# A recurrent cell's state products from fp16 parts, theta computed earlier, two sums merged, preparation reordered

## The chip, the cores and the metric

The kernel runs on one core of a Trainium2 chip. Its time is the device time of one execution, in microseconds (us), as a median over runs. The core has five engines that run their own instruction streams and wait for each other through semaphores: TensorE (PE, its weight loads shown as PEld), VectorE (DVE), ScalarE (ACT), GpSimd (POOL) and SyncE (SP), which issues most DMAs.

## The reference

2048 sequences of 256 steps go through a recurrent cell. In each step, with the carried state `st` (32 values), error, gate (8 values), a memory of the last 20 inputs and two LSTM cells:

```python
encoded = jnp.tanh(xt @ We + st @ Ue + be)
new_state = jnp.tanh(jnp.einsum('bd,cds->bcs', xt, Wx) + jnp.einsum('bs,cst->bct', st, Ws) + bk)
inp = jnp.concatenate([encoded, err[:, None]], axis=1)
mem = jnp.concatenate([inp[:, None, :], mem[:, :-1, :]], axis=1)
a = jax.nn.relu(mem.reshape(b, -1) @ enc_w1 + enc_b1)
agent_in = jax.nn.relu(a @ enc_w2 + enc_b2)
h1, c1 = _lstm_cell(agent_in, h1, c1, ...)
h2, c2 = _lstm_cell(h1, h2, c2, ...)
gate = jax.nn.softmax(h2 @ gate_w + gate_b, axis=1)
theta = _clamp01(jnp.mean(jnp.abs(mem[:, :10, -1]), axis=1) * 2.5)[:, None]
gate = gate * theta + gs * (1.0 - theta)
st = jnp.einsum('bc,bcs->bs', gate, new_state)
pred = _clamp01(st[:, -1])
err = pred - yt
```

The output is `pred` of every step, as fp32.

## The kernel before

The 2048 sequences are cut into two groups of 1024, a group into eight tiles of 128 sequences (`HF` 2 by `Q` 4). A work item is one step of one group, so there are 512 items. The engines handle them in phases, one new item in each: `run_phases` keeps the last three items, called new, cur and old, and each engine's `phase` function does its part of all three in a fixed, hand-written order. An engine runs its list strictly in that order. The first two items and the last two phases lie outside a loop of 51 turns with five steps of both groups (ten phases) each.

What an item goes through, with the lines at which it is recorded:

- TensorE transposes the state (`state_transpose`, L293, two matmuls) and the prediction (L305), ScalarE copies the state to SBUF (`state_take`, L498), TensorE adds W_e's and U_e's products (`encoded_x` L320, `encoded_s` L327), and ScalarE makes the encoded input and its fp16 high part (L504, L511); GpSimd makes the low part (`entry_low`, L944), which SyncE stores in the history.
- The first encoder layer is `history` (L378, fp16 parts) and `encoder1_now` (L389), the second is L400. Two LSTM cells follow: products `cell_gates` (L417), ScalarE's tanhs (L550, L555, L560), VectorE's `cell_terms` (L705), `cell_value` (L711), `first_hidden` (L720, two instructions) and `second_hidden` (L729).
- The candidates of the new state get their bias (L340), x's part from fp16 pieces that GpSimd splits (`x_high` L933, `x_low` L938; products L350, 24 of them: weight high by x high, weight low by x high, weight high by x low) and the state's part in fp32 (L359: eight products, recorded as 16). ScalarE takes their tanh (`candidates`, L536, one instruction for each quarter).
- The logits (L427, L434) go to VectorE (`peaks` L752, `below_peak` L757), ScalarE (L574), VectorE (`totals`, `reciprocals`) and GpSimd (`weighted_exponentials`, L891, which multiplies by theta), then `fresh_gate` (L774) and `new_gate` (L781) on VectorE and `gate_in_sbuf` (L899) on GpSimd. Theta comes from `error_sum` (L681) and `thetas` (L687); GpSimd makes 1-theta and the kept part of the old gate from it (`kept_share` L877, `kept_gate` L884).
- The mix of candidates by the gate is split: VectorE multiplies half of it (L792), GpSimd two quarters of it (`mix_quarter` 1, then 0, L911). VectorE sums over the candidates in four `mix_sum` (L810), clamps the prediction (`prediction`, L818), and GpSimd forms the new error (`new_error`, L968) and keeps the prediction (`keep_prediction`, L977).

VectorE's order in a phase: totals, reciprocals, fresh_gate, new_gate (old); agent_input (cur); mix, sum (old); cell_terms 0, cell_value 0 (cur); sum (old); first_hidden (cur); two sums (old); error_sum (cur); prediction (old); cell_terms 1, cell_value 1 (cur); errors (new); second_hidden, thetas, peaks, below_peak (cur). GpSimd's order: gate_in_sbuf, two mix quarters (old); x_high, x_low (new); next_hidden (L921, old); kept_share, kept_gate (cur); new_error, keep_prediction (old); entry_low (new); weighted_exponentials (cur). `x_high` waits for `first_hidden` by choice, to keep away from VectorE's work.

Before the first item VectorE splits biases (L637 to L641) and the history's weight table (L647, L648) into fp16 parts, scales weights and marks the preparation as done (L676). SyncE then issues the first three sets of history weights (L223), without which TensorE can't start.

Of the kernel before, what the change touches and what calls it, by code (L numbers as in the profile page):

```python
# [41 lines left out]
def recurrent_kernel(nc, x_l, y_l, y, error0, gate0, w, ident_c, columns_c, out):  # L42
    ctx = ExitStack()
    with ctx:
# [18 lines left out]
        w_s = sb("w_s", [P, NS])  # L63
        w_x_parts = sb("w_x_parts", [P, 2, NS], FP16)
# [12 lines left out]
        ones = sb("ones", [P, TILES])  # L77

# [47 lines left out]
        s_out, s_ys, s_hist0 = sem("s_out"), sem("s_ys"), sem("s_history_zero")  # L126
        s_x = [sem(f"s_x_slot{u}") for u in range(PER_TILE)]
# [22 lines left out]
        q_xh, q_xl = sem("q_xh"), sem("q_xl")  # L150
        q_bias = [sem(f"q_bias{c}") for c in range(2)]
        q_hkept = sem("q_hkept")
        q_sum = [[sem(f"q_sum{hf}_{pair}") for pair in range(2)] for hf in range(HF)]
# [45 lines left out]
        def _(sp):  # L199
# [11 lines left out]
            for t in range(PER_TILE):  # L211
                sp.dma_start(x_sb[:, t, :, :].rearrange("p g b -> p (g b)"), x_l[P * t:P * t + P, :])\
                    .then_inc(s_x[t], 16)
                sp.dma_start(y_rows[0:Q, t, :, :].rearrange("p g b -> p (g b)"), y_l[Q * t:Q * t + Q, :])\
                    .then_inc(s_y[t], 16)


            sp.wait_ge(s_parts, 1)
            sp.dma_start(gate_bias[1:2, :], gate_bias_low[0:1, :]).then_inc(s_fix, 16)
            sp.dma_start(cand_bias[1:P:D_IN, :], cand_bias_low[0:P:D_IN, :]).then_inc(s_fix, 16)  # L220
# [6 lines left out]
            sp.wait_ge(s_ready, 1)  # L227
            history_weights(w_slot(-1), PER_TILE)
            history_weights(0, PER_TILE + 1)
            history_weights(1, PER_TILE + 2)  # L230

# [53 lines left out]
        def _(pe):  # L285
            pe.wait_ge(s_ready, 1)
            pe.wait_ge(s_fix, 16 * 2)

            def state_transpose(item, hf):
                g, n, u = item  # L290
                for pair in range(2):
                    pe.wait_ge(q_sum[hf][pair], n)
# [41 lines left out]
            def candidates_bias(item):  # L334
                g, n, u = item
                for q in CAND_ORDER:
                    pe.wait_ge(q_cand[q], n)
# [16 lines left out]
            def candidates_s(item):  # L354
                g, n, u = item
                for hf in range(HF):
                    for q in range(Q):
                        rows = slice(D_IN * q, D_IN * q + D_IN)
                        last = nc.tensor.matmul(cand_ps[q][:, NS * hf:NS * hf + NS],  # L359
                                                state_t[rows, g, P * hf:P * hf + P], w_s[rows, :],  # L360
                                                start=False, stop=True, skip_group_check=True)
# [82 lines left out]
            def phase(items, extra):  # L444
# [21 lines left out]
                if cur:  # L466
                    cell_gates(cur, 0)
                    candidates_bias(cur)
# [11 lines left out]
        def _(act):  # L480
# [11 lines left out]
            act.dma_start(ys[:, :, :], y.rearrange("(n p) t -> p n t", p=P)).then_inc(s_ys, 16)  # L492
            act.wait_ge(s_ready, 1)
# [115 lines left out]
        def _(dve):  # L609
            V = nc.vector  # L610
            V.memset(err_ring[:, :, :], 0.5).then_inc(s_zero, 1)

# [10 lines left out]
            for hf in range(HF):  # L623
                for pair in range(2):
                    V.memset(state[:, :, hf, 2 * pair:2 * pair + 2, :], 0.0).then_inc(q_sum[hf][pair], GROUPS)
            V.memset(scratch[:, :, :], 0.0).then_inc(s_prep, 1)
            dve.wait_ge(s_prep, 1)
            dve.wait_ge(s_biases, 16 * 2)
# [3 lines left out]
            def link(ins):  # L632
# [4 lines left out]
            link(V.tensor_copy(cand_bias[:, :], bk_stage))  # L637
            link(V.tensor_tensor(cand_bias_low[:, :], bk_stage, cand_bias[:, :], ALU.subtract))

            link(V.tensor_copy(gate_bias[0:1, :], gate_bias_stage[0:1, :]))  # L640
            V.tensor_tensor(gate_bias_low[0:1, :], gate_bias_stage[0:1, :], gate_bias[0:1, :], ALU.subtract)\  # L641
                .then_inc(s_parts, 1)

# [6 lines left out]

# [9 lines left out]
            link(V.tensor_scalar(cell_bias[:, :, 0:3], cell_bias[:, :, 0:3], 0.5, None, ALU.mult))  # L660
            link(V.tensor_copy(w_x_parts[:, 0, :], w_x[:, :]))
# [14 lines left out]
            V.tensor_copy(scratch[:, 1, :], ones[:, :]).then_inc(s_ready, 1)  # L676

# [134 lines left out]

            def prediction(item):
                g, n, u = item
                for hf in range(HF):
                    for pair in range(2):
                        dve.wait_ge(q_sum[hf][pair], n + GROUPS)
# [6 lines left out]
            def phase(items, extra):  # L824
# [19 lines left out]
                if old:  # L844
                    mix_sum(old, 1, 0)
                    mix_sum(old, 1, 1)
# [4 lines left out]
                if cur:  # L851
                    cell_terms(cur, 1)
# [6 lines left out]
                if cur:  # L859
                    second_hidden(cur)  # L860
                    thetas(cur)
# [6 lines left out]
        def _(pool):  # L868
# [71 lines left out]

            def entry_low(item):
# [44 lines left out]
            def phase(items, extra):  # L986
# [114 lines left out]
```

## Time and profile before

| | us |
|---|---|
| median of 3 runs | 5336.49 (5336.03 to 5337.18) |
| profiled execution | 5342.21 |
| its span | 5340.3 |
| granted TensorE clock, share of full speed | 0.998 |
| busy: PE, DVE, ACT, POOL | 5165.0, 4468.2, 4233.4, 3060.8 |

The profile is of one execution. Its span runs from the first to the last instruction of the program; the execution's own time is a little longer. A busy share counts the time in which an engine works on instructions; matmuls overlap, and their ends are modelled, so two rows of TensorE can overlap. A timeline row gives the start in us from the span's start, the duration, the engine and line, the operation, what it writes and reads, and how many instructions the row merges; in brackets stands how long the engine was idle ahead of it, and for whom it waited.

### The profile page before, as it was taken

The page shows a single profiled execution, that of the slowest core. Times are in us where ns is not written, and L with a number is a line of the kernel's source. Part 1 is how long each engine was busy: PE and PEld are TensorE (multiplying, and loading weights), DVE is VectorE, ACT ScalarE, POOL GpSimd, SP SyncE. Part 2 cuts the span into 40 slices and gives each one's busy share as a digit, 9 for nine tenths or more (in the row PEclk, how much of TensorE's full clock was granted, in tenths as well). Part 3 has the DMA queues.
Part 4 walks back from the last instruction along what each step waited for, and adds up shares of the span by engine and source line. Part 5 has one row for each costly group of instructions (what it writes and reads, how often), then busy time and mean ns, then how long its engine had stood idle before and what let it go on. Part 6 is the DMA issues. An engine that isn't in the chain of part 4 may idle for free.

```text
span 5340.3 us, 193942 instructions
## 1 busy us (share of the span) xinstructions
PE 5165.0 (97%) x68608; PEld 3158.5 (59%) x68608; DVE 4468.2 (84%) x11824; ACT 4233.4 (79%) x10241; POOL 3060.8 (57%) x6149
## 2 busy tenths in 40 slices
PE   7999999999999999999999999999999999999998
PEld 4555555555555555555555555555555555555554
DVE  7888888888888888888888888888888888888887
ACT  6887877878888878788787788788877878777886
POOL 4555555555555555555555555555555555555555
PEclk9999999999999999999999999999999999999999
DMA  2111111111111111111111111111111111111111
GB/s 68 31 30 33 30 33 30 33 30 33 30 33 30 31 31 30 33 30 33 30 33 30 33 30 33 30 32 30 30 33 30 33 30 33 30 33 30 33 30 41
DMA packets 299271, 172.29 MB, mean 32 GB/s; under 512 B 156598, under 2 KB 263866, under 8 KB 298698
## 3 DMA queue, kind: packets, MB, share of 16 engines
q1 hardware_dynamic: 293560, 159.45, 11.9%
q8 instruction: 564, 9.24, 0.7%
q10 hardware_dynamic: 5138, 3.53, 0.2%
q14 instruction: 9, 0.07, 0.0%
HBM read 74.55 MB, written 2.10 MB: 14 GB/s over the span
## 4 chain that ended last, share of the span: by engine, by line
PE 94%; ACT 4%; issue 2%; DVE 0%; DMA 0%; POOL 0%; ACTq 0%; POOLq 0%; DVEq 0%
PE a_ps L378 27%; PE chain L417 21%; PE a_ps L389 9%; PE cand_ps L359 8%; PE cand_ps L350 6%; PE chain L327 6%; PE chain L320 4%; ACT state_t L498 4%; PE chain L293 4%; PE a_ps L400 3%; PE cand_ps L340 3%; PE chain L434 1%; PE chain L427 0%; DMA gate_bias_stage<-in_gate_b 0%; DVE enc_table L648 0%
## 5 line engine op out<-in xcount | busy, mean ns | idle before, releaser
L378 PE MATMUL a_ps<-hist,w_hist 125*64 125x512 f16 x12288 | 1816.5, 383 | 25.2 <-DMA w_hist<-enc_table 24.0
L810 DVE TENSOR_REDUCE state<-mixed 128x64 f32<-128x512 f32 x2048 | 1353.4, 682 | 34.2 <-POOL mixed L911 0.8
L911 POOL TENSOR_TENSOR mixed<-cand,gate 128x512 f32<-128x512 f32 x1024 | 1285.3, 1277 | 48.6 <-POOL gate L899 12.5
L417 PEld LDWEIGHTS chain<-cell_in,cell_w 128*64 128x64 f32 x16384 | 903.2, 136 | 488.7 <-ACT cell_in L525 248.5
L417 PE MATMUL chain<-cell_in,cell_w 128*64 128x128 f32 x16384 | 1120.5, 277 | 41.5 <-issue 1.4
L536 ACT ACTIVATE cand<-cand_ps 128x512 f32<-128x512 f32 x2048 | 1107.0, 594 | 13.3 <-issue 0.4
L378 PEld LDWEIGHTS a_ps<-hist,w_hist 125*64 125x64 f16 x12288 | 695.8, 109 | 568.8 <-issue 298.1
L933 POOL CAST x_parts<-x_sb 128x256 f16<-128x256 f32 x512 | 203.8, 398 | 953.2 <-DVE cell_in L720 938.4
L550 ACT ACTIVATE gates<-chain 128x384 f32<-128x384 f32 x1024 | 503.5, 492 | 251.2 <-PE chain L417 251.2
L705 DVE SCALAR_TENSOR_TENSOR added<-gates 128x256 f32<-128x256 f32 x1024 | 620.8, 606 | 57.2 <-ACT gates L550 3.7
L877 POOL TENSOR_TENSOR one_theta<-ones,theta 128x8 f32<-128x8 f32 x512 | 105.3, 206 | 950.0 <-DVE theta L687 950.0
L543 ACT ACTIVATE chain<-cell_bias 128x512 f32<-128x512 f32 x1024 | 611.0, 597 | 16.1
L792 DVE TENSOR_TENSOR mixed<-cand,chain 128x1024 f32<-128x1024 f32 x512 | 616.4, 1204 | 0.2 <-issue 0.2
L560 ACT ACTIVATE tanh_c<-gates 128x128 f32<-128x128 f32 x1024 | 318.8, 311 | 305.1 <-DVE gates L711 305.0
L389 PE MATMUL a_ps<-entry,w_now 100*64 100x256 f32 x4096 | 555.0, 388 | 0.0
L359 PE MATMUL cand_ps<-w_s,state_t 32*128 32x256 f32 x8192 | 529.3, 375 | 0.0
L350 PE MATMUL cand_ps<-w_x_parts,x_parts 32*128 32x256 f16 x12288 | 421.5, 268 | 0.0
L327 PE MATMUL chain<-state_t,w_ue 128*64 128x256 f32 x2048 | 334.1, 405 | 87.4 <-ACT state_t L498 87.1
L517 ACT ACTIVATE a_sb<-a_ps,columns 128x512 f32<-128x512 f32 x512 | 352.3, 688 | 69.6 <-PE a_ps L389 0.8
L359 PEld LDWEIGHTS cand_ps<-w_s,state_t 32*128 32x128 f32 x8192 | 356.5, 186 | 24.7
L938 POOL TENSOR_TENSOR x_parts<-x_sb,x_parts 128x256 f16<-128x256 f32 x512 | 344.6, 673 | 41.1
L350 PEld LDWEIGHTS cand_ps<-w_x_parts,x_parts 32*128 32x128 f16 x12288 | 315.7, 93 | 71.7
(80 smaller groups left out, 7348.5 us busy)
## 6 DMA issues: line engine op xcount, KB each, us to landing
x_sb<-in_x_l SPq DMA_DIRECT2D x260, 256.0 KB, 2.7
hist<-entry_parts SPq DMA_DIRECT2D x2048, 25.0 KB
w_hist<-enc_table SPq DMA_DIRECT2D x258, 128.0 KB, 2.4
y_rows<-in_y_l SPq DMA_DIRECT2D x260, 8.0 KB
ys<-in_y ACTq DMA_DIRECT2D x1, 2048.0 KB, 16.7
preds_out<-preds SPq DMA_DIRECT2D x1, 2048.0 KB, 7.5
cand<-in_encoder ACTq DMA_DIRECT2D x1, 640.0 KB, 3.8
cell_w<-in_cell ACTq DMA_DIRECT2D x2, 256.0 KB, 5.3
```

Of the source, the lines that this page charges most:

```text
L327: last = nc.tensor.matmul(chain[g][rows, Z_AT:Z_AT + COLS], w_ue[:, rows], state_t[:, g, :], start=False, stop=True, skip_group_check=True)
L350: nc.tensor.matmul(cand_ps[q][:, NS * hf:NS * hf + NS], x_parts[rows, g, xp, P * hf:P * hf + P], w_x_parts[rows, wp, :], start=False, stop ...
L359: last = nc.tensor.matmul(cand_ps[q][:, NS * hf:NS * hf + NS], state_t[rows, g, P * hf:P * hf + P], w_s[rows, :], start=False, stop=True, ...
L378: nc.tensor.matmul(a_ps[g][ENC * half:ENC * half + ENC, :], w_hist[0:HROWS, w_slot(u), kk, wp, :], hist[0:HROWS, xp, k, at:at + 512], star ...
L389: last = nc.tensor.matmul(a_ps[g][rows, COLS * p:COLS * p + COLS], w_now[0:ER, p, rows], entry[0:ER, g, :], start=False, stop=True, skip_g ...
L417: last = nc.tensor.matmul(chain[g][rows, P * r:P * r + P], cell_w[c][:, hf, r, :], cell_in[c][:, g, hf, :], start=False, stop=True, skip_g ...
L536: ins = nc.scalar.activation(cand[:, g, q // 2, :, q % 2, :, :].rearrange("p h s c -> p h (s c)"), cand_ps[q][:, :].rearrange("p (h k) -> ...
L543: nc.scalar.activation(chain[g][:, :].rearrange("p (r b) -> p r b", r=4), cell_bias[:, c, :].rearrange("p (r o) -> p r o", o=1).to_broadca ...
L705: V.scalar_tensor_tensor(added[c][:, g, :, :], gates[c][:, g, 1:3, :], 1.0, gates[c][:, g, 3:5, :], ALU.add, ALU.mult).then_inc(q_added[c], 1)
L792: V.tensor_tensor(mixed[:, 1, :, :, :, :].rearrange("p h l s c -> p (h l) s c"), cand[:, g, 1, :, :, :, :].rearrange("p h l s c -> p (h l) ...
L810: V.tensor_reduce(state[:, g, hf, 2 * pair:2 * pair + 2, :], mixed[:, pair, hf, :, :, :], AX, ALU.add)\
L911: G.tensor_tensor(mixed[:, 0, :, q, :, :], cand[:, g, 0, :, q, :, :], over_s, ALU.mult)\
```

## The change

Six edits. The state's part of the candidates uses fp16 pieces: `w_s` is split once, and for each item GpSimd makes a high and a low part of the transposed state (`state_high`, `state_low`); TensorE does 24 fp16 products in place of the fp32 ones and waits for the low part. `thetas` stands directly behind `prediction` on VectorE. GpSimd's `new_error` and `keep_prediction` stand ahead of `kept_share` and `kept_gate`, and the two new functions come after these, ahead of `entry_low`. The last two sums of an item are one instruction, `last_sums`. In the preparation the history weights' DMAs are issued as soon as their table is split, x and y of slots 1 to 4 and the bias rows behind them; the biases are split after the mark, and only the first candidates wait for them. ScalarE does a small Tanh before it waits for the mark.

```diff
@@ tiles and semaphores
+        w_s_parts = sb("w_s_parts", [P, 2, NS], FP16)
+        state_parts = sb("state_parts", [P, GROUPS, 2, COLS], FP16)
+        warm = sb("warm", [P, 2, TILES])
-        q_sum = [[sem(f"q_sum{hf}_{pair}") for pair in range(2)] for hf in range(HF)]
+        q_sum = [[sem(f"q_sum0_{pair}") for pair in range(2)], [sem("q_sum1")]]
@@ sync
-            sp.wait_ge(s_parts, 1)
-            sp.dma_start(gate_bias[1:2, :], gate_bias_low[0:1, :]).then_inc(s_fix, 16)
-            sp.dma_start(cand_bias[1:P:D_IN, :], cand_bias_low[0:P:D_IN, :]).then_inc(s_fix, 16)
-            sp.wait_ge(s_ready, 1)
+            load_slot(0)
+            sp.wait_ge(s_tables, 1)
             history_weights(w_slot(-1), PER_TILE)
             history_weights(0, PER_TILE + 1)
             history_weights(1, PER_TILE + 2)
+            for t in range(1, PER_TILE):
+                load_slot(t)
+            sp.wait_ge(s_parts, 1)
+            sp.dma_start(gate_bias[1:2, :], gate_bias_low[0:1, :]).then_inc(s_fix, 16)
+            sp.dma_start(cand_bias[1:P:D_IN, :], cand_bias_low[0:P:D_IN, :]).then_inc(s_fix, 16)
+            sp.wait_ge(s_ready, 1)
@@ tensor
             pe.wait_ge(s_ready, 1)
-            pe.wait_ge(s_fix, 16 * 2)
-            def candidates_bias(item):
+            def candidates_bias(item, extra):
                 g, n, u = item
+                if extra is None:
+                    pe.wait_ge(s_fix, 16 * 2)
             def candidates_s(item):
                 g, n, u = item
+                pe.wait_ge(q_sl, n)
                 for hf in range(HF):
-                    for q in range(Q):
-                        rows = slice(D_IN * q, D_IN * q + D_IN)
-                        last = nc.tensor.matmul(cand_ps[q][:, NS * hf:NS * hf + NS],
-                                                state_t[rows, g, P * hf:P * hf + P], w_s[rows, :],
-                                                start=False, stop=True, skip_group_check=True)
+                    for t, (wp, xp) in enumerate(PIECES):
+                        for q in range(Q):
+                            rows = slice(D_IN * q, D_IN * q + D_IN)
+                            last = nc.tensor.matmul(cand_ps[q][:, NS * hf:NS * hf + NS],
+                                                    state_parts[rows, g, xp, P * hf:P * hf + P],
+                                                    w_s_parts[rows, wp, :], start=False,
+                                                    stop=(t == len(PIECES) - 1), skip_group_check=True)
@@ scalar, before the wait for s_ready
+            act.wait_ge(s_warm, 1)
+            nc.scalar.activation(warm[:, 1, :], warm[:, 0, :], ACT.Tanh)
@@ vector, preparation (the four bias instructions now stand behind s_ready)
+            V.tensor_copy(scratch[:, 1, :], ones[:, :]).then_inc(s_tables, 1)
...
+            link(V.tensor_copy(w_s_parts[:, 0, :], w_s[:, :]))
+            link(V.tensor_tensor(w_s_parts[:, 1, :], w_s[:, :], w_s_parts[:, 0, :], ALU.subtract))
@@ vector
+            def last_sums(item):
+                g, n, u = item
+                dve.wait_ge(q_mul[1], n + GROUPS)
+                for q in range(2):
+                    dve.wait_ge(q_mulpool[q], n + GROUPS)
+                V.tensor_reduce(state[:, g, 1, :, :].rearrange("p (a l) s -> p a (l s)", a=2),
+                                mixed[:, :, 1, :, :, :].rearrange("p a l s c -> p a (l s) c"), AX, ALU.add)\
+                    .then_inc(q_sum[1][0], 1)
@@ vector, phase
                 if old:
-                    mix_sum(old, 1, 0)
-                    mix_sum(old, 1, 1)
+                    last_sums(old)
                 if cur:
                     error_sum(cur)
                 if old:
                     prediction(old)
                 if cur:
+                    thetas(cur)
                     cell_terms(cur, 1)
...
                     second_hidden(cur)
-                    thetas(cur)
                     peaks(cur)
@@ gpsimd
+            def state_high(item):
+                g, n, u = item
+                pool.wait_ge(s_ready, 1)
+                pool.wait_ge(q_st, n)
+                G.tensor_copy(state_parts[:, g, 0, :], state_t[:, g, :]).then_inc(q_sh, 1)
+
+            def state_low(item, other):
+                g, n, u = item
+                pool.wait_ge(q_sh, n)
+                if other:
+                    pool.wait_ge(q_h[1], n - 1)
+                G.tensor_tensor(state_parts[:, g, 1, :], state_t[:, g, :], state_parts[:, g, 0, :],
+                                ALU.subtract).then_inc(q_sl, 1)
@@ gpsimd, phase
                 if old:
                     next_hidden(old, cur)
+                    new_error(old, extra)
+                    keep_prediction(old, extra)
                 if cur:
                     kept_share(cur)
                     kept_gate(cur)
-                if old:
-                    new_error(old, extra)
-                    keep_prediction(old, extra)
+                if new:
+                    state_high(new)
+                    state_low(new, cur)
                 if new:
                     entry_low(new)
```

## Rows read from the trace of the kernel before

**Rows 1.** The page, busy time by engine.
```profile
PE 5165.0 (97%) x68608; PEld 3158.5 (59%) x68608; DVE 4468.2 (84%) x11824; ACT 4233.4 (79%) x10241; POOL 3060.8 (57%) x6149
```
**Rows 2.** Timeline of TensorE, two phases of the loop; start and duration in us.
```profile
2157.78 0.44 PE L293 MATMUL chain<-ident,state 128*128 128x128 f32 x2
...
2159.85 0.32 PE L434 MATMUL chain<-gate_w,h_second 128*64 128x64 f32 x4
...
2166.22 0.60 PE L320 MATMUL chain<-x_sb,w_we 128*64 128x256 f32 x4
2166.86 1.09 PE L417 MATMUL chain<-cell_in,cell_w 128*64 128x128 f32 x16
...
2168.10 0.44 PE L293 MATMUL chain<-ident,state 128*128 128x128 f32 x2
...
2178.38 0.44 PE L293 MATMUL chain<-ident,state 128*128 128x128 f32 x2
```
**Rows 3.** The chain of waits in the first of them; start, length.
```profile
2164.31 0.65 PE cand_ps L350 x24
2164.97 0.87 PE cand_ps L359 x16
...
2166.39 0.43 PE chain L320 x4
```
**Rows 4.** Timeline of VectorE, the same phases.
```profile
2157.88 0.20 DVE L818 TENSOR_SCALAR pred_now<-state 128x8 f32<-128x8 f32 x1
2158.19 0.42 DVE L705 SCALAR_TENSOR_TENSOR added<-gates 128x256 f32<-128x256 f32 x1
...
2159.49 0.29 DVE L729 SCALAR_TENSOR_TENSOR h_second<-gates,tanh_c 128x128 f32<-128x128 f32 x1
2159.70 0.17 DVE L687 TENSOR_SCALAR theta<-err_sum 128x8 f32<-128x8 f32 x1
...
2161.81 0.23 DVE L774 TENSOR_TENSOR fresh<-weighted,recip 128x64 f32<-128x64 f32 x1 [0.33 <-POOL weighted L891]
2162.07 0.23 DVE L781 TENSOR_TENSOR chain<-fresh,kept 128x64 f32<-128x64 f32 x1
...
2164.55 0.79 DVE L705 SCALAR_TENSOR_TENSOR added<-gates 128x256 f32<-128x256 f32 x1
...
2166.18 0.57 DVE L720 SCALAR_TENSOR_TENSOR cell_in<-gates,tanh_c 64x128 f32<-64x128 f32 x2
2166.79 1.28 DVE L810 TENSOR_REDUCE state<-mixed 128x64 f32<-128x512 f32 x2
...
2174.88 0.74 DVE L705 SCALAR_TENSOR_TENSOR added<-gates 128x256 f32<-128x256 f32 x1
```
**Rows 5.** Timeline of GpSimd, the same phases.
```profile
2157.66 0.40 POOL L921 COPY cell_in<-cell_in 128x256 f32<-128x256 f32 x1
...
2160.78 0.67 POOL L944 TENSOR_TENSOR entry_parts<-entry,entry_parts 128x256 f16<-128x256 f32 x1
2161.41 0.30 POOL L891 TENSOR_TENSOR weighted<-expd,theta 128x64 f32<-128x64 f32 x1
2162.11 0.36 POOL L899 TENSOR_TENSOR gate<-fresh,kept 128x64 f32<-128x64 f32 x1 [0.41 <-DVE fresh L774]
2162.55 2.51 POOL L911 TENSOR_TENSOR mixed<-cand,gate 128x512 f32<-128x512 f32 x2
...
2172.83 2.51 POOL L911 TENSOR_TENSOR mixed<-cand,gate 128x512 f32<-128x512 f32 x2
```
**Rows 6.** Timeline of ScalarE, candidate 0 in the first phase.
```profile
2162.82 0.60 ACT L536 ACTIVATE cand<-cand_ps 128x512 f32<-128x512 f32 x1
```
**Rows 7.** Timeline of the first 35 us: mark, first products, table load.
```profile
21.23 0.16 DVE L676 COPY scratch<-ones 128x8 f32<-128x8 f32 x1
...
24.01 3.62 PE L378 MATMUL a_ps<-hist,w_hist 125*64 125x512 f16 x16 [24.01 <-DMA w_hist<-enc_table]
...
29.45 1.28 ACT L498 ACT_TABLE_LOAD   x1 [29.45 <-PE chain L293]
```

More of the change, by code:

```diff
@@ L126, in recurrent_kernel @@
         s_out, s_ys, s_hist0 = sem("s_out"), sem("s_ys"), sem("s_history_zero")
+        s_tables, s_warm = sem("s_tables"), sem("s_warm")
         s_x = [sem(f"s_x_slot{u}") for u in range(PER_TILE)]
@@ L150, in recurrent_kernel @@
         q_xh, q_xl = sem("q_xh"), sem("q_xl")
+        q_sh, q_sl = sem("q_sh"), sem("q_sl")
         q_bias = [sem(f"q_bias{c}") for c in range(2)]
         q_hkept = sem("q_hkept")
-        q_sum = [[sem(f"q_sum{hf}_{pair}") for pair in range(2)] for hf in range(HF)]
+        q_sum = [[sem(f"q_sum0_{pair}") for pair in range(2)], [sem("q_sum1")]]
         block = ctx.enter_context(nc.Block())
@@ L210, in _, with load_slot @@
                 load(err_ring[:, :, 0:1], error0.rearrange("(n p o) -> p n o", p=P, o=1))
-            for t in range(PER_TILE):
+            def load_slot(t):
                 sp.dma_start(x_sb[:, t, :, :].rearrange("p g b -> p (g b)"), x_l[P * t:P * t + P, :])\
@@ L286, in _ @@
             pe.wait_ge(s_ready, 1)
-            pe.wait_ge(s_fix, 16 * 2)
             def state_transpose(item, hf):
                 g, n, u = item
-                for pair in range(2):
-                    pe.wait_ge(q_sum[hf][pair], n)
+                for done in q_sum[hf]:
+                    pe.wait_ge(done, n)
                 last = nc.tensor.matmul(chain[g][:, P * hf:P * hf + P],
@@ L467, in phase @@
                     cell_gates(cur, 0)
-                    candidates_bias(cur)
+                    candidates_bias(cur, extra)
                     candidates_x(cur)
@@ L610, in _ @@
             V = nc.vector
+            V.memset(warm[:, 0, :], 0.0).then_inc(s_warm, 1)
             V.memset(err_ring[:, :, :], 0.5).then_inc(s_zero, 1)
@@ L622, in _ @@
                 V.memset(gates[n][:, :, 4, :], 0.0)
-            for hf in range(HF):
-                for pair in range(2):
-                    V.memset(state[:, :, hf, 2 * pair:2 * pair + 2, :], 0.0).then_inc(q_sum[hf][pair], GROUPS)
+            for pair in range(2):
+                V.memset(state[:, :, 0, 2 * pair:2 * pair + 2, :], 0.0).then_inc(q_sum[0][pair], GROUPS)
+            V.memset(state[:, :, 1, :, :], 0.0).then_inc(q_sum[1][0], GROUPS)
             V.memset(scratch[:, :, :], 0.0).then_inc(s_prep, 1)
             dve.wait_ge(s_prep, 1)
-            dve.wait_ge(s_biases, 16 * 2)
             steps = [1]
@@ L635, in link @@
                 dve.wait_ge(s_prep, steps[0])
[L637 to L642, printed above, removed]
             dve.wait_ge(s_table, 16)
@@ L676, in _ @@
             V.tensor_copy(scratch[:, 1, :], ones[:, :]).then_inc(s_ready, 1)
+            dve.wait_ge(s_biases, 16 * 2)
+            link(V.tensor_copy(cand_bias[:, :], bk_stage))
+            link(V.tensor_tensor(cand_bias_low[:, :], bk_stage, cand_bias[:, :], ALU.subtract))
+            link(V.tensor_copy(gate_bias[0:1, :], gate_bias_stage[0:1, :]))
+            V.tensor_tensor(gate_bias_low[0:1, :], gate_bias_stage[0:1, :], gate_bias[0:1, :], ALU.subtract)\
+                .then_inc(s_parts, 1)
             def error_sum(item):
@@ L815, in prediction @@
                 for hf in range(HF):
-                    for pair in range(2):
-                        dve.wait_ge(q_sum[hf][pair], n + GROUPS)
+                    for done in q_sum[hf]:
+                        dve.wait_ge(done, n + GROUPS)
                 V.tensor_scalar(pred_now[:, g, :].rearrange("p (h q) -> p h q", h=HF), state[:, g, :, :, S - 1],
```

## The prediction

> **What bounds the kernel now.** I read the page's busy shares first, then the chain of waits, then the timelines of the four engines over two phases of the steady loop, then the first 30 us. A phase is one work item of one group: 512 of them, each about 10.3 us. The page calls TensorE 97% busy [rows 1] and the chain runs through matmuls almost alone, so at first sight every nanosecond of TensorE counts. The timelines say otherwise. Take the phase that starts with the state transpose at 2157.78 and ends with the next at 2168.10 (10.32 us), and the one after it, to 2178.38 (10.28 us) [rows 2]. I give times as offsets from the phase's start.
>
> Near its end stand four W_e products (L320), begun at 8.44; they take 0.43 [rows 2, 3], so TensorE could go on at 8.87. The second cell's products (L417) begin only at 9.08 [rows 2]. They wait for `first_hidden` (L720) on VectorE, which ends at 8.97 (2166.18+0.57) [rows 4]; 0.11 later the products start, and 1.24 after them the next transpose [rows 2]. That gap of 0.21 is invisible in the chain, because modelled ends of matmuls cover it. Why does L720 end then? VectorE runs in order from `cell_terms` of cell 0 (L705): in the middle of the phase it takes 0.79, not the 0.42 of the same instruction at 2158.19 [rows 4]. It ends at 2165.34, 0.28 after GpSimd's two mixes (2162.55+2.51 = 2165.06) [rows 4, 5]. In the next phase: mixes end at 2175.34, L705 at 2175.62, again 0.28, while its duration is another (0.74). So L705, which reads two SBUF operands, stands still until GpSimd's mix is done, and then runs its whole stream. The cycle is then: mix end + 0.28 + 1.41 (L705's end to L720's) + 0.11 + 1.24 = mix end + 3.04. It gives 2168.10 and 2178.38, exactly both transposes [rows 2]. What sets the time is when GpSimd finishes the mixes.
>
> The Trainium skill (Trainium Kernel Development and Optimization, Performance Expectations) says that matmul busy time is a bad metric of distance from the roof because matmuls are pipelined. The trace agrees: 97% busy, and 0.21 of each phase is a pause. By the opposite reading the change would bring the full saving of its matmuls, which is rival 1.
>
> Going back from the mixes: they start 0.74 after `fresh_gate` (L774) does (2161.81 to 2162.55), and L774 starts 0.10 after GpSimd's `weighted_exponentials` (L891, 3.63 to 3.93) [rows 4, 5]. L891 is late because theta comes late: VectorE makes it (L687) only behind `second_hidden`, at 1.92, and behind it GpSimd has five instructions in a row up to L944, the subtraction (0.67) that ends at 3.67 [rows 4, 5].
>
> **The change, part by part.**
> *State products in fp16.* Out: the 0.87 of L359. In: 24 fp16 products of the same tiles as L350's, 0.65 [rows 3]. TensorE saves 0.22 a phase. By itself this only widens the pause. Its new wait for the low part delays nothing: the state's parts are ready by about 2.8 (below) and the products start at 7. Behind this wait everything of TensorE would queue, with 4 us of cover.
>
> *Theta behind the prediction.* Theta (0.17) falls between `prediction` (L818, which ends at 0.30) and L705 at 0.41 [rows 4]; L687 starts 0.08 before its predecessor ends, as at 2159.70, so it is done at 0.39 and L705, which waits for ScalarE's gates, isn't moved. Its cover is this gap; without it the cost would be 0.17 at most. Nothing is waiting on VectorE at its old place (it waits for logits there).
>
> *GpSimd's queue.* The six instructions from `kept_share` to `weighted` stood behind theta (done at 2.09). Now `new_error` starts at 0.30+0.08 = 0.38, then `keep_prediction`, then theta's two, at about 0.15, 0.15, 0.3 from start to start, all before 1.5 instead of from 2.16 on. Added: the fp16 copy of the state (0.40, as L921 for 256 elements) and the subtraction (0.67, as L944) [rows 5]. The copy waits for the state at about 0.86 and then the queue, and runs at 1.45 to 1.85. The subtraction waits for `second_hidden` (end 2.00 [rows 4]) and starts 0.08 after it. Behind these two waits stand `entry_low` and `weighted`.
>
> *Collisions.* What the new order adds is GpSimd work during `cell_terms`, `cell_value` and `second_hidden`, which all read two SBUF operands. `new_error` starts at 0.38, L705 at 0.41 [rows 4]. By the 0.28 rule just read, L705 ends at 0.60+0.28 = 0.88 instead of 0.83: +0.05. The trace has no short GpSimd instruction under such an L705, so the bounds are 0 (the small ones hold nothing) and 0.34 (rival 4). The reverse also occurs: `gate_in_sbuf` (L899), begun 0.04 after `new_gate` (L781), takes 0.36 where L891 of the same shape takes 0.30 [rows 4, 5]; whoever starts first holds the other. I take 0.05. Then `second_hidden` ends at 2.05 and the logits (L434 at 2.07 [rows 2]) start 0.07 after it, at 2.12.
> The Trainium skill (SBUF — State Buffer, Who interferes with whom) has this rule: a VectorE instruction with two SBUF inputs contends with a GpSimd instruction that reads SBUF, and the one issued first has the shared ports for its whole duration. It speaks against this change, which puts four more such instructions there; by it L705 would lose what remains of `new_error`, near the 0.05 taken from the rows.
>
> *Sum.* State subtraction 2.13; `entry_low` 0.63 later (pitch of L944 to L891 [rows 5]) at 2.76; `weighted` at 3.39 to 3.69; `fresh_gate` at 3.79 instead of 4.03; the mixes 4.53 to 7.04. The second mix (half of 2.51 and a little, 1.28) also needs candidate 0, which ScalarE (L536) ends at 5.64 [rows 6], 5.69 behind the later logits, and 0.08 more to GpSimd: not before 5.77, end 7.05. So this floor is just reached, and earlier weights would bring nothing more. Mix end: 7.28 becomes 7.05; phase: 10.09, a gain of 0.23. In the other phase of the pair the mixes start at 4.73 [rows 2, 5], 0.04 earlier; it meets the floor at 10.05, gain 0.23 too. TensorE's own road is now 8.87-0.22+1.24 = 9.89, below both; with L359 left in fp32 it would be 10.11, so the fp16 split is what lets the last 0.02 to 0.06 be had.
> 512 x 0.23 = 118 us.
>
> *Last two sums in one.* Two take 1.28 [rows 4]. One of 1024 elements: between 1.20 (one start less, an estimate) and 1.28; taken 1.21. They end 0.1 before TensorE asks, so 0 on the path.
>
> *Preparation.* The history weights are now issued once the tables are split, not behind the final mark (L676, done at 21.39), so TensorE, which began at 24.01 when they landed [rows 7], can begin near 21.4: -2.6. Bias splitting goes behind the mark, fp16 parts of W_s come before it; I take these as equal. The eight DMAs of x and y slots 1 to 4 go behind the weights, their first use is a phase or more later. The two bias DMAs come after the mark and have some 10 us until the first candidates. An early Tanh moves the table load (1.28 [rows 7]) under the loads: -1.3. Together -4, bounds 0 and -7.
>
> Total: -118 - 4 = -122. The profiled execution took 5342.2 (span 5340.3), so it would become 5220; it lies 5.7 above the median shown, 5336.5, and from that the forecast is 5215.
>
> **Rivals.**
> 1. *TensorE is the bound after all.* For it: 97% busy and the chain. Against: the pause of 0.21 and the exact 3.04. 512 x 0.22 = 113, with preparation 5220; the steps of GpSimd would then not matter. The time hardly differs from mine, the trace would.
> 2. *No collisions.* Short instructions hold nothing. Both phases stand at the floor of candidate 0, 5.72+1.28+3.04 = 10.04: gain 0.28 and 0.24, mean 0.26: 133+4, 5200.
> 3. *The gain is eaten by waiting in GpSimd's queue.* If L705 gets in first (a margin of 0.03), `new_error` waits until 0.83, each of the next waits for the next VectorE instruction, the copy of the state runs against `second_hidden` and ends near 2.3, and `weighted` ends near 3.92, where it was (3.93). Gain 0: 5332. A middle case: the copy gets in first, holds `second_hidden` until about 2.2, and the gain sinks to 0.08: 41+4, 5291.
> 4. *Slower: VectorE is held behind the whole string.* GpSimd's four short instructions follow each other without a gap; if the waiting L705 can't get in between, it ends at about 0.90+0.28 = 1.18, `second_hidden` at 2.34 and the logits start at 2.41, +0.34 (0.27 in the other phase), and GpSimd's road goes on from there: subtraction 2.42, `entry_low` 3.05, `weighted` 3.68 to 3.98, `fresh_gate` 4.08, mix end 7.33, phase 10.37 against 10.32 (10.31 against 10.28 in the other). 512 x 0.04 = 20, less 4: 5352. It is slower than before from a hold of about 0.3 on. For it: GpSimd's records overlap by 0.06. Against: the instruction that has waited longest should be next.
>
> **Chances.** Forecast 0.42; rival 1 0.11; rival 2 0.14; rival 3 0.13 at no gain, 0.10 in the middle; rival 4 0.10. A measurement of this kernel can tell 0.2% (10.7 us) from nothing: faster (below 5325.8) 0.42+0.11+0.14+0.10 = 0.77, within it 0.13, slower 0.10. The range: from 5190 (below rival 2, with a preparation of -7 and rounding) up to 5335, since without the case of no gain 0.23 would be left out. The likeliest case alone: 5200 to 5240.
>
> **What would show it.** In the profile after: phases of about 10.07; the mixes ending at about 7.0 and L705 still 0.28 behind them; `weighted` ending near 3.7; the first L705 0.47 rather than 0.42; GpSimd's second mix starting 0.08 behind candidate 0; TensorE still pausing before L417. Wrong: L705 of cell 1 over 0.6, or `second_hidden` past 2.1 (rival 4, middle case); `weighted` at 3.9 (rival 3); no pause before L417 at a shorter phase (rival 1).

## The result, and the profile after

The changed kernel takes 5296.3 us (5296.1 to 5296.6, 4 runs) against 5336.8 before: ratio 0.9924, interval 0.9907 to 0.9942. It is faster by 40 us where 122 were forecast. The profiled execution's span is 5294.5 instead of 5340.3, 45.8 less; that is more than 40 because the profiled execution of the kernel before took 5342.2, 5.4 more than its median here. In the span, the first state transpose comes 3.3 us earlier (25.5 instead of 28.8), and the 511 distances from transpose to transpose are 10.246 us on average instead of 10.331: 43.4 us. Of these, 1.6 come from the first distance alone (9.92 instead of 11.50). The stretch behind the last transpose is 1.0 longer. Averages over the loop in this text are taken over 472 of its phases in a run's trace.

The page's busy time by engine, as [rows 1]:

```profile
PE 5097.5 (96%) x72704; PEld 2994.3 (57%) x72704; DVE 4465.8 (84%) x11315; ACT 4215.9 (80%) x10242; POOL 3684.6 (70%) x7173
```

TensorE has 67 us less of busy time and GpSimd 624 more. Neither number is near 40. One phase tells more; it starts at 2156.75 (TensorE's timeline, as [rows 2]; lines have moved, L428 is the cells' products, L299 the state's transpose, L369 the new fp16 products):

```profile
2156.75 0.44 PE L299 MATMUL chain<-ident,state 128*128 128x128 f32 x2
...
2158.96 0.34 PE L445 MATMUL chain<-gate_w,h_second 128*64 128x64 f32 x4
...
2163.87 0.82 PE L369 MATMUL cand_ps<-w_s_parts,state_parts 32*128 32x256 f16 x24
...
2165.08 0.60 PE L326 MATMUL chain<-x_sb,w_we 128*64 128x256 f32 x4
2165.75 1.09 PE L428 MATMUL chain<-cell_in,cell_w 128*64 128x128 f32 x16
2166.99 0.44 PE L299 MATMUL chain<-ident,state 128*128 128x128 f32 x2
```

The logits (L445) start 2.21 after the phase's start, not at 2.07 as before. The fp16 products are as cheap as forecast: their 0.82 above includes overlap, and in the chain of waits they take 0.66, where the fp32 ones took 0.87 [rows 3]:

```profile
2164.04 0.66 PE cand_ps L369 x24
```

Yet L428 still waits: L326's 0.43 end at 2165.51, L428 starts at 2165.75, a pause of 0.24 (0.21 before). VectorE's timeline, as [rows 4] (L720 is `cell_terms`, L842 `prediction`, L702 theta, L744 `second_hidden`, L735 `first_hidden`):

```profile
2156.79 0.26 DVE L842 TENSOR_SCALAR pred_now<-state 128x8 f32<-128x8 f32 x1
2156.97 0.16 DVE L702 TENSOR_SCALAR theta<-err_sum 128x8 f32<-128x8 f32 x1
2157.16 0.43 DVE L720 SCALAR_TENSOR_TENSOR added<-gates 128x256 f32<-128x256 f32 x1
...
2158.47 0.44 DVE L744 SCALAR_TENSOR_TENSOR h_second<-gates,tanh_c 128x128 f32<-128x128 f32 x1
...
2163.63 0.61 DVE L720 SCALAR_TENSOR_TENSOR added<-gates 128x256 f32<-128x256 f32 x1
```

and GpSimd's, as [rows 5] (L1005 `new_error`, L968 and L975 the state's copy and subtraction, L914 `weighted_exponentials`, L934 the mixes):

```profile
2157.27 0.40 POOL L1005 TENSOR_TENSOR err_ring<-pred_now,ys 128x8 f32 x1 [0.24 <-DVE pred_now L842]
2157.61 0.20 POOL L1014 COPY preds<-pred_now 128x8 f32 x1
2157.76 0.29 POOL L900 TENSOR_TENSOR one_theta<-ones,theta 128x8 f32<-128x8 f32 x1
2158.13 0.29 POOL L907 TENSOR_TENSOR kept<-gate,one_theta 128x64 f32<-128x64 f32 x1
2158.36 0.40 POOL L968 CAST state_parts<-state_t 128x256 f16<-128x256 f32 x1
2159.05 0.67 POOL L975 TENSOR_TENSOR state_parts<-state_t,state_parts 128x256 f16<-128x256 f32 x1 [0.29 <-DVE h_second L744]
2159.68 0.67 POOL L981 TENSOR_TENSOR entry_parts<-entry,entry_parts 128x256 f16<-128x256 f32 x1
2160.31 0.29 POOL L914 TENSOR_TENSOR weighted<-expd,theta 128x64 f32<-128x64 f32 x1
2161.01 0.36 POOL L922 TENSOR_TENSOR gate<-fresh,kept 128x64 f32<-128x64 f32 x1 [0.41 <-DVE fresh L789]
2161.45 2.51 POOL L934 TENSOR_TENSOR mixed<-cand,gate 128x512 f32<-128x512 f32 x2
```

The cycle is the one read before: mixes end at 2163.96, `cell_terms` 0.28 later (2164.24, held again: 0.61), the next transpose 3.03 after the mixes' end. But `new_error` starts at 0.52 of the phase, not 0.38, so `cell_terms` (0.41) comes first and is not held (0.43), while `new_error` takes 0.40 instead of 0.22. It ends 0.07 after `cell_terms`, and it does so in the whole loop, in the four phases of five where it starts 0.21 behind the prediction as in the fifth, where it starts 0.32 behind: once it comes second, its own start no longer counts. GpSimd's string is that much later, the state's copy runs from 2158.36 to 2158.76, and `second_hidden`, begun at 2158.47, stands until then: 0.44 instead of 0.29. It ends 0.15 after the copy, in every phase of the loop. That moves the logits by 0.14 (0.11 on average over the loop), and the state's subtraction, which waits for `second_hidden`, with them. The rows show this hold; what it is worth, and what each part of the change does, the runs below tell.

### The profile page after: what moved, and what is told of

Same layout as the page of the kernel before. It is cut to its first block, busy times and chain, and to the rows that moved or that the text cites. A ratio compares the mean times of both kernels' runs of the same rounds, so it can differ in the third digit from the quotient of the medians.

```text
span 5294.5 us, 202648 instructions
## 1 busy us (share of the span) xinstructions
PE 5097.5 (96%) x72704; PEld 2994.3 (57%) x72704; DVE 4465.8 (84%) x11315; ACT 4215.9 (80%) x10242; POOL 3684.6 (70%) x7173
## 4 chain that ended last, share of the span: by engine, by line
PE 93%; ACT 4%; issue 2%; DVE 0%; POOL 0%; DMA 0%; POOLq 0%; DVEq 0%; ACTq 0%
PE a_ps L389 27%; PE chain L428 21%; PE a_ps L400 8%; PE cand_ps L358 6%; PE cand_ps L369 6%; PE chain L333 6%; PE chain L326 4%; ACT state_t L511 4%; PE chain L299 4%; PE a_ps L411 3%; PE cand_ps L348 3%; PE chain L445 3%; PE chain L438 0%; DVE enc_table L653 0%; DMA cand<-in_encoder 0%
## 5 line engine op out<-in xcount | busy, mean ns | idle before, releaser
L934 POOL TENSOR_TENSOR mixed<-cand,gate 128x512 f32<-128x512 f32 x1024 | 1283.6, 1275 | 51.4 <-POOL gate L922 12.8
L428 PEld LDWEIGHTS chain<-cell_in,cell_w 128*64 128x64 f32 x16384 | 904.0, 136 | 516.5 <-issue 268.2
L428 PE MATMUL chain<-cell_in,cell_w 128*64 128x128 f32 x16384 | 1121.3, 277 | 67.0 <-issue 13.7
L389 PEld LDWEIGHTS a_ps<-hist,w_hist 125*64 125x64 f16 x12288 | 637.5, 109 | 562.8 <-issue 212.0
L825 DVE TENSOR_REDUCE state<-mixed 128x64 f32<-128x512 f32 x1024 | 698.4, 682 | 19.6 <-POOL mixed L934 1.9
L833 DVE TENSOR_REDUCE state<-mixed 128x128 f32<-128x1024 f32 x512 | 624.7, 1220 | 15.8
L720 DVE SCALAR_TENSOR_TENSOR added<-gates 128x256 f32<-128x256 f32 x1024 | 540.5, 528 | 21.2 <-ACT gates L563 4.0
L400 PE MATMUL a_ps<-entry,w_now 100*64 100x256 f32 x4096 | 530.9, 379 | 0.0
L975 POOL TENSOR_TENSOR state_parts<-state_t,state_parts 128x256 f16<-128x256 f32 x512 | 344.1, 672 | 149.2 <-DVE h_second L744 149.1
L369 PE MATMUL cand_ps<-w_s_parts,state_parts 32*128 32x256 f16 x12288 | 421.7, 268 | 0.0
```

What stands on the lines that cost most here:

```text
L389: nc.tensor.matmul(a_ps[g][ENC * half:ENC * half + ENC, :], w_hist[0:HROWS, w_slot(u), kk, wp, :], hist[0:HROWS, xp, k, at:at + 512], star ...
L400: last = nc.tensor.matmul(a_ps[g][rows, COLS * p:COLS * p + COLS], w_now[0:ER, p, rows], entry[0:ER, g, :], start=False, stop=True, skip_g ...
L428: last = nc.tensor.matmul(chain[g][rows, P * r:P * r + P], cell_w[c][:, hf, r, :], cell_in[c][:, g, hf, :], start=False, stop=True, skip_g ...
L825: V.tensor_reduce(state[:, g, hf, 2 * pair:2 * pair + 2, :], mixed[:, pair, hf, :, :, :], AX, ALU.add)\
L833: V.tensor_reduce(state[:, g, 1, :, :].rearrange("p (a l) s -> p a (l s)", a=2), mixed[:, :, 1, :, :, :].rearrange("p a l s c -> p a (l s) ...
L934: G.tensor_tensor(mixed[:, 0, :, q, :, :], cand[:, g, 0, :, q, :, :], over_s, ALU.mult)\
```

## The experiments

Every run is given with the median of the kernel before that was measured with it. These medians differ by up to 6 us, on one chip too, so runs are compared by their ratios. No run is numbered e8.

| run | us | before | ratio (interval) |
|---|---|---|---|
| changed kernel | 5296.3 | 5336.8 | 0.9924 (0.9907 to 0.9942) |
| e1, state in fp32 | 5219.4 | 5340.9 | 0.9773 (0.9757 to 0.9790) |
| e2, a third of the products | 5324.7 | 5340.9 | 0.9968 (0.9956 to 0.9979) |
| e3, copy on ScalarE | 5229.3 | 5340.9 | 0.9792 (0.9775 to 0.9808) |
| e4, copy behind second_hidden | 5472.7 | 5340.9 | 1.0247 (1.0230 to 1.0264) |
| e5, short mix (on the kernel before) | 5210.2 | 5336.0 | 0.9762 (0.9746 to 0.9779) |
| e6, theta back | 5735.4 | 5336.0 | 1.0746 (1.0729 to 1.0764) |
| e7, fixed address | 5237.1 | 5336.0 | 0.9812 (0.9796 to 0.9829) |
| e9, e3 with one wait | 5221.4 | 5336.0 | 0.9784 (0.9767 to 0.9800) |
| e10, e9 with candidate 0 early | 5196.7 | 5342.0 | 0.9729 (0.9716 to 0.9743) |
| e11, e1 with candidate 0 early | 5252.0 | 5342.0 | 0.9834 (0.9821 to 0.9848) |
| e12, preparation and sums only | 5336.4 | 5342.0 | 0.9990 (0.9981 to 0.9999) |

**e5: is it the end of the mixes?** In the kernel before, half of GpSimd's second mix is left out; these products stay zero.

```diff
+            V.memset(mixed[:, :, :, :, :, :].rearrange("p a h l s c -> p (a h l s c)"), 0.0)
...
-                over_s = gate[:, g, q:Q:2, :]...to_broadcast([P, HF, S, C])
-                G.tensor_tensor(mixed[:, 0, :, q, :, :], cand[:, g, 0, :, q, :, :], over_s, ALU.mult)
+                some = HF if q == 1 else 1
+                over_s = gate[:, g, q:q + 2 * some - 1:2, :]...to_broadcast([P, some, S, C])
+                G.tensor_tensor(mixed[:, 0, 0:some, q, :, :], cand[:, g, 0, 0:some, q, :, :], over_s, ALU.mult)
```


> The kernel before the change, with half of GpSimd's second mix left out (quarter 0 of one half; these products stay zero). Its mixes end 0.6 us earlier in each phase, TensorE's work is untouched. Theory (the mix's end releases VectorE's cell_terms and sets the phase): cell_terms of cell 0 runs in 0.42 us and the phase falls from 10.33 us to TensorE's own road, 10.09 as the fp32 run showed: 5341 - 123 = about 5218. Rival (TensorE's matmuls bind): no change, 5341.

5210, ratio 0.9762. TensorE's work is that of the kernel before, and 126 us are gone. GpSimd's timeline, the short second mix, VectorE's `cell_terms` after it, and TensorE's products:

```profile
2149.82 0.72 POOL L913 TENSOR_TENSOR mixed<-cand,gate 128x256 f32<-128x256 f32 x1
```
```profile
2150.53 0.41 DVE L706 SCALAR_TENSOR_TENSOR added<-gates 128x256 f32<-128x256 f32 x1
```
```profile
2152.20 0.60 PE L320 MATMUL chain<-x_sb,w_we 128*64 128x256 f32 x4
2152.63 1.04 PE L417 MATMUL chain<-cell_in,cell_w 128*64 128x128 f32 x16
```

The mix ends at 2150.54 and `cell_terms` isn't held. L417 follows L320 after 0.43, without a pause. The mean phase is 10.070, now TensorE's own road with fp32 products. So the 97% of [rows 1] hid a wait.

**e2: is it TensorE?** 16 of the 24 state products are left out.

```diff
-                    for t, (wp, xp) in enumerate(PIECES):
+                    for t, (wp, xp) in enumerate(PIECES[:1]):
...
-                                                    stop=(t == len(PIECES) - 1), skip_group_check=True)
+                                                    stop=(t == 0), skip_group_check=True)
```


> The changed kernel with 16 of the 24 state products of each item left out (only high by high is computed), which takes 0.43 us a phase from TensorE. Theory: TensorE is not the bound, it pauses longer before the second cell's products; 5296 within 5. Rival (TensorE is the bound): 512 x 0.43 = 220 us less, about 5076.

5325, slower than the changed kernel, not faster. Eight of ten phases of a loop turn are as long as there (10.25 and 10.22). TensorE's waits (in total, times, longest) show the pause before the second cell's products, which lies open here, at 0.52 in every phase:

```profile
PE chain L428 <- issue: 265.3, 511, 0.7
```

The tenth, at the turn's end, takes 10.79 on average instead of 10.29, and the one behind it 10.19 instead of 10.33: 0.36 a turn, 18 us in 51 turns. That is the loss of the profiled execution (5313.9), the fastest of seven; the other six lie between 5322 and 5325, and for what they lose beyond it there is no trace. At the turn's end the transpose comes up to 3.95 behind the mixes' end and not 3.04, so there TensorE is late by itself. Why the turn's end costs more with fewer instructions in it was not found out.

**e1: the split undone.** The fp32 products are back, and `state_high` and `state_low` are gone:

```diff
-                pe.wait_ge(q_sl, n)
...
-                if new:
-                    state_high(new)
-                    state_low(new, cur)
```


> The changed kernel with one part undone: the state's products in fp32 again (0.87 us a phase on TensorE instead of 0.65), and GpSimd neither copies nor subtracts the state. Theory (the time is set by when GpSimd ends its mixes, and the fp16 copy of the state holds second_hidden for 0.15 us a phase): second_hidden ends at 2.00 again, weighted_exponentials at 3.6, GpSimd's second mix starts at its floor behind candidate 0 (5.72 us after the phase's start) and ends at 7.00; the cycle over the mixes is 10.04 us, TensorE's own road with fp32 10.11. Phase about 10.12 instead of 10.25: 5296 - 65 = about 5232. Rival (TensorE's work is the bound): 512 x 0.22 us come back, about 5408.

5219, ratio 0.9773: the split costs this kernel 1.5%, and what is left, theta's place with GpSimd's new order, brings 2.2% (e1 less the 0.1% of e12). How much of it is theta's place and how much GpSimd's order was not run apart. Nothing holds `second_hidden` (0.29), and `weighted_exponentials` ends 0.24 earlier on average over the loop. GpSimd's and TensorE's timelines:

```profile
2150.14 2.58 POOL L931 TENSOR_TENSOR mixed<-cand,gate 128x512 f32<-128x512 f32 x2
```
```profile
2155.76 0.44 PE L299 MATMUL chain<-ident,state 128*128 128x128 f32 x2
```

The next transpose is 3.04 behind the mixes' end (2152.72). The two mixes take 2.58, not 2.51: the second waits for candidate 0, so this is the floor, 10.088 in nine of ten phases. It lies 0.02 above TensorE's own road with fp32 products, 10.07 in e5; the prediction had put that road at 10.11.

**e4 and e6: GpSimd's queue.** In e4 the copy waits for `second_hidden` too; in e6 theta is back at its old place.

```diff
                 pool.wait_ge(q_st, n)
+                if other:
+                    pool.wait_ge(q_h[1], n - 1)
```


> The changed kernel, but GpSimd's fp16 copy of the state also waits for second_hidden, so it can't hold it. Theory (both the hold and GpSimd's queue up to weighted_exponentials count): second_hidden at 2.00, but copy and subtraction follow it, weighted_exponentials ends at about 4.18 instead of 3.85 us after the phase's start, mixes at 7.53, phase 10.57: 5296 + 165 = about 5460. Rival (the hold is the whole loss): 0.13 us a phase less, about 5229.


```diff
-                    thetas(cur)
                     cell_terms(cur, 1)
...
                     second_hidden(cur)
+                    thetas(cur)
```


> The changed kernel with one part undone: thetas stands behind second_hidden again, all else as changed. Theory (GpSimd's queue up to weighted_exponentials sets the mixes): one_theta starts at 2.17 us of the phase, kept at 2.45, copy and subtraction of the state 2.7 to 3.85, weighted ends at 4.73 instead of 3.85, mixes at 8.1, phase 11.1: 5296 + 450 = about 5750. Rival (theta's place is worth no more than its 0.17 us on VectorE): 5296 within 20.

5473 and 5735, both within 15 of the expectation. In e4 nothing holds `second_hidden`, and still the phase is 10.59, because `weighted_exponentials` comes 0.35 later. The hold alone is thus not what counts; the queue up to `weighted_exponentials` is. In e6 the string of six stands behind theta (GpSimd's timeline):

```profile
2160.17 0.21 POOL L900 TENSOR_TENSOR one_theta<-ones,theta 128x8 f32<-128x8 f32 x1 [1.12 <-DVE theta L702]
...
2162.43 0.30 POOL L914 TENSOR_TENSOR weighted<-expd,theta 128x64 f32<-128x64 f32 x1
```

With all parts of the change but theta's move, the kernel is thus 7.5% slower than before: the parts are far from additive.

**e7: the step that failed.** `new_error` with constant columns and one wait, so that GpSimd computes no address behind the wait. It follows neither the ring nor the step.

```diff
                 pool.wait_ge(q_pred, n + GROUPS)
-                pool.wait_ge(q_errsum, n)
...
-                G.tensor_tensor(by_quarter(err_ring[:, tiles, bass.ds(ring, 1)]), pred,
-                                by_quarter(ys[:, tiles, bass.ds(step, 1)]), ALU.subtract)
+                G.tensor_tensor(by_quarter(err_ring[:, tiles, 0:1]), pred,
+                                by_quarter(ys[:, tiles, 0:1]), ALU.subtract)
```


> The changed kernel, but new_error reads and writes fixed columns (the error's ring and the step are not followed) and waits for the prediction alone, so that GpSimd computes no address behind the wait: it starts at about 0.38 us of the phase instead of 0.52, ahead of cell_terms (0.41), as the prediction had it. Theory (what failed was the order in which the two reach the shared operand path): cell_terms is now held until new_error ends (0.60) and ends at 0.88, the fp16 copy of the state runs at 1.45 to 1.85, second_hidden isn't held and ends at 2.05 instead of 2.15, weighted_exponentials ends at 3.69 instead of 3.85; phase 10.09 instead of 10.23: 5296 - 72 = about 5224. Rival (VectorE goes first whatever starts first, and the copy still holds second_hidden): 5296.

5237, ratio 0.9812. GpSimd's timeline, then VectorE's:

```profile
2154.70 0.21 POOL L1004 TENSOR_TENSOR err_ring<-pred_now,ys 128x8 f32<-128x8 f32 x1
2154.85 0.39 POOL L1013 COPY preds<-pred_now 128x8 f32 x1
...
2155.72 0.40 POOL L968 CAST state_parts<-state_t 128x256 f16<-128x256 f32 x1
```
```profile
2154.72 0.46 DVE L720 SCALAR_TENSOR_TENSOR added<-gates 128x256 f32<-128x256 f32 x1
...
2156.06 0.29 DVE L744 SCALAR_TENSOR_TENSOR h_second<-gates,tanh_c 128x128 f32<-128x128 f32 x1
```

Now `new_error` is 0.02 ahead, ends at 2154.91, and `cell_terms` ends at 2155.18, 0.27 later: held for 0.04. The copy ends at 2156.12 and `second_hidden` has its 0.29. The edit moves `new_error`'s start by 0.14 and turns the order round, and it is the order that counts: in the changed kernel `new_error` ends 0.07 behind `cell_terms` from either of its two starts. So which of two instructions comes first, here by 0.02 to 0.03, is worth 59 us. The rule read from the long mixes holds for an instruction of eight elements too. The run takes away a wait and the computed address at once; which of them made `new_error` late was not run apart. It is 13 above its forecast: the mean phase is 10.137, not 10.09.

**e3, e9, e10: a better kernel.** ScalarE makes the state's copy (e3), the subtraction waits for one semaphore (e9), candidate 0 is taken in ScalarE's gap ahead of the second cell (e10):

```diff
+            def state_high(item):
+                g, n, u = item
+                act.wait_ge(q_st, n)
+                nc.scalar.activation(state_parts[:, g, 0, :], state_t[:, g, :], ACT.Copy).then_inc(q_sh, 1)
...
                     cell_tanh_out(cur, 1)
+                if new:
+                    state_high(new)
@@ gpsimd, phase
                 if new:
-                    state_high(new)
                     state_low(new, cur)
```


> The changed kernel, but ScalarE makes the fp16 copy of the state, between cell_tanh_out and value_tanh; GpSimd only subtracts, after second_hidden. Theory: nothing holds second_hidden (2.02 instead of 2.15 us after the phase's start, 0.02 lost to ScalarE), weighted_exponentials ends at 3.6 instead of 3.85, the mixes at 7.0 instead of 7.2, phase 10.05: 5296 - 100 = about 5197. Rival A (TensorE is the bound): no change, 5296. Rival B (ScalarE's extra 0.4 us delays the cell's tanh and the encoded input by their full length): second_hidden at 2.4, about 5400.


```diff
-                pool.wait_ge(q_sh, n)
                 if other:
                     pool.wait_ge(q_h[1], n - 1)
+                else:
+                    pool.wait_ge(q_sh, n)
```


> As the run with the copy of the state on ScalarE, and GpSimd's subtraction waits for second_hidden alone (which comes behind the copy), not for two semaphores. Theory: the subtraction starts 0.08 us behind second_hidden instead of 0.14, weighted ends at 3.64 instead of 3.70, the mixes at 7.02, phase 10.05 instead of 10.10: 0.05 x 512 = 25 us less than that run's 5229, about 5204. Rival (the wait's form costs nothing): 5229.


```diff
                     candidates(cur, 3)
                     candidates(cur, 1)
+                    candidates(cur, 0)
...
-                    candidates(cur, 0)
```


> As the one-wait run (copy of the state on ScalarE), and ScalarE takes candidate 0 right behind candidates 3 and 1, in the 0.5 us in which it waits for the second cell, not behind the next item's agent input. Theory: there the phase (10.09) was at the floor of candidate 0, whose end at 5.64 let the second mix start only at 5.77; now the mixes run back to back from 4.48 to 6.99 and the phase is 6.99 + 3.04 = 10.03: 512 x 0.055 = 28 us under that run's 5221, about 5193. Rival A (the floor is TensorE's or another road): 5221. Rival B (the moved tanh delays the second cell's by 0.1): about 5270.

5229, 5221 and 5197. ScalarE's extra 0.42 cost nothing in e3. e3 was forecast at 5197 and missed: the subtraction starts 0.14, not 0.08, behind `second_hidden`, and the phase of 10.05 that was forecast lies below candidate 0's floor. e9 mends the first, but then stands at that floor, 10.09 as e1, and so its mean phases are worth 10 us and not 25 (the intervals of e3 and e9 overlap, so the times alone don't show a gain). With the same phase and the same time as e1, e9 also shows that the split need not cost anything. With candidate 0 early the mixes run back to back (GpSimd's timeline of e10, then TensorE's):

```profile
2150.00 2.50 POOL L942 TENSOR_TENSOR mixed<-cand,gate 128x512 f32<-128x512 f32 x2 [0.25 <-POOL gate L930]
```
```profile
2155.53 0.44 PE L299 MATMUL chain<-ident,state 128*128 128x128 f32 x2
```

Mix end + 3.03 again, nine of ten phases at 10.03. It beats both kernels: 2.7% under before, 2.0% under the change.

**e11: candidate 0 early with fp32 products.** The same move on e1.

> The same move of candidate 0 in the kernel with the state's products in fp32 (GpSimd makes no parts of the state). Theory: the mixes would allow 10.03, but TensorE's own road with fp32 products is 10.067, as the short-mix run showed; only here does the fp16 split pay, 0.03 a phase. Against the fp32 run (5219 with a before of 5341, so 5215 with one of 5336) 512 x 0.02 = 10 less: about 5205, some 12 above its fp16 counterpart. Rival (TensorE never binds): as the fp16 counterpart, 5193.

5252, where 5205 was forecast, and slower than e1: what rival B of e10 says came true here. The fp32 products end 0.2 later, so ScalarE's four tanhs begin later and run into the second cell's. ScalarE's timeline:

```profile
2157.88 2.06 ACT L546 ACTIVATE cand<-cand_ps 128x512 f32<-128x512 f32 x4
2159.81 0.52 ACT L560 ACTIVATE gates<-chain 128x384 f32<-128x384 f32 x1
```

L560, the second cell's first tanh, starts right behind them, on average 0.08 later in the phase than in e10; `cell_terms` starts at 0.52 instead of 0.41, in 58% of the phases behind `new_error`, and `second_hidden` ends at 2.11 instead of 1.98. The mixes' end still sets the phase (mix end + 3.04). Only from here on does the fp16 split pay, because its products end earlier and so let ScalarE start earlier: e10 against e11 is 1.1%.

**e12: preparation and sums alone.**

> The kernel before with only two of the parts of the change: the reordered preparation (with the early Tanh) and the last two sums in one. Theory: the loop stays at its 10.33 us because GpSimd's mixes end where they did; the preparation is 3.3 us shorter, as the changed kernel's first transpose shows: 5336 - 3 = about 5333. Rival (the merged sum is on the path): 512 x 0.07 = 36 less, about 5297.

5336.4 against 5342.0, ratio 0.9990, 5.6 us. The spans differ by 5.9: 3.2 before the first transpose, 1.1 in the first distance from transpose to transpose, 0.8 in the other 510, and 0.7 at the end. The merged sum takes 1.22 (forecast: 1.21) and is off the path; the phase is 10.33.

## Why the prediction was wrong

- *What bounds the kernel*: right. The end of GpSimd's mixes sets the phase, by mix end + 3.04 on average in before, after, e1, e4, e6 and e10 alike; e5 and e2 exclude TensorE (rival 1).
- *Fp16 products*: TensorE's saving right, its effect wrong in sign. "What lets the last 0.02 to 0.06 be had" was nothing: TensorE's road with fp32 is 10.07 (e5) and not 10.11, so the forecast's phases didn't need the split, and e1, with fp32, is 0.15 a phase shorter than the change, since GpSimd pays for the parts.
- *Theta*: right in kind. With GpSimd's new order it brings 2.2% (e1), and without it the rest is 7.5% slower than before (e6).
- *Collisions*: this step failed. The prediction had "`new_error` starts at 0.38, L705 at 0.41", taking 0.08 from VectorE's end to GpSimd's start. That held in e7, where `new_error` waits once and has a fixed address; in the changed kernel it waits for two semaphores and computes an address, starts 0.21 behind VectorE's end, and so at 0.52. The order turned round, the copy ran into `second_hidden`, and the middle case of rival 3 came about, which I had at 5291 and 0.10: `second_hidden` at 2.16 (said: about 2.2, and past 2.1 as its sign), gain 0.085 (said: 0.08). e7 turns the order back and gets 5237.
- *The other 22 us*, from 5215 up to 5237: e7's loop gains 0.194 a phase and not 0.23, which is 18 of them. On average its subtraction starts 0.14 and not 0.08 behind `second_hidden`, `weighted_exponentials` ends at 3.72 (said: 3.69), and the mixes start at 4.58 (said: 4.53) and end at 7.09 (said: 7.05). They run back to back in 2.50, so candidate 0's floor doesn't bind there. Where it does, in e1 and e9, the second mix starts 0.13 behind candidate 0, not 0.08.
- *Sums, preparation*: right. The sums bring 0; before the first transpose and in the first distance behind it the changed kernel gains 3.3 + 1.6 us and e12 3.2 + 1.1, where 4 were said.
- Rival 4, VectorE shut out by the whole string, didn't occur, but the changed kernel never tested it, since VectorE came first; in e7 it was let in right behind `new_error`, before `keep_prediction`.

## What to carry to other kernels

A 97% busy engine can be waiting: look for a distance that stays the same from another engine's end to its next start, in phases of different length. Work given to a second engine is paid for in that engine's queue, and on GpSimd also in VectorE's instructions with two SBUF operands, whoever starts first. Where two such streams meet within a tenth of a microsecond or so, a forecast must price both orders.

## What the runs showed of the hardware

- A VectorE instruction with two SBUF operands that meets a running GpSimd one ends a fixed time after it: 0.28 for 256 elements behind a product of 512 elements (all kernels in which it meets one), 0.27 behind a subtraction of 8 (e7), and 0.15 for 128 behind the copy of 256 (changed kernel). GpSimd, coming second, waits likewise: `new_error` takes up to 0.40 instead of 0.22 and ends 0.07 behind `cell_terms`. The Trainium skill (SBUF — State Buffer, Who interferes with whom) says that issue order decides who blocks, and, of VectorE's two-port modes, that the other fully blocks; by e7 and the changed kernel the trace agrees with both for VectorE instructions with two SBUF inputs.
- From VectorE's end to GpSimd's start: `new_error` 0.08 with one wait and a fixed address (e7), 0.21 in four phases of five and 0.32 in the fifth with two waits and a computed address (changed kernel); the state's subtraction 0.08 with one wait (e9), 0.14 with two (e3). The number of waits isn't the whole rule: `gate_in_sbuf` waits for two semaphores as well, the late one first, and starts 0.08 to 0.13 behind `fresh_gate` in every run. What decides among these was not run.
